# A graph layer in float32 pieces: whole transfers at the start, evacuations ahead of low parts in the first items, the last degrees in fours, W at an item's end, the epilogue one item later

## What is computed

```python
d   = (sum(adj, axis=1) + 1e-9) ** -0.5            # adj 4096 x 4096, degrees by row
H_f = relu((d[:, None] * adj * d[None, :] @ x) @ W_f + b_f)          # x 4096 x 128
H_s = relu((d[:, None] * adj * d[None, :] @ spatial_x) @ W_s + b_s)
a   = sigmoid(concat(H_f, H_s) @ W_att + b_att)    # one number per row
out = layernorm(x + a * H_f + (1 - a) * H_s)       # over the 128 columns
```

## Time and profile before

| | |
|---|---|
| Median of 3 runs | 442.38 us |
| The profiled execution | 443.2 us, its span 441.4 us |
| TensorE | busy 382.8 us (87%), granted clock 0.955 on average |
| VectorE, ScalarE, GpSimd | busy 295.1, 277.8, 200.7 us |
| Transfers | 128.65 MB, mean 291 GB/s; 0.11 MB and 0.21 MB of it instructions |

### The profile page before, as it was taken

How to read it: one execution, slowest core, us unless ns; L and a number is a source line. 1 busy time by engine, 2 the same in 40 slices (tenths; PEclk the granted TensorE clock), 3 DMA queues, 4 the chain that set the end, 5 groups by cost and what they waited for, 6 DMA issues and landing times.

```text
span 441.4 us, 5188 instructions
## 1 busy us (share of the span) xinstructions
PE 382.8 (87%) x1680; PEld 313.5 (71%) x1680; DVE 295.1 (67%) x376; ACT 277.8 (63%) x338; POOL 200.7 (45%) x246
## 2 busy tenths in 40 slices
PE   0699996989979999999999999959999967889850
PEld 0477884868868887888788878748888847768740
DVE  2379957278566957686659834567555775966764
ACT  3778588787577759788888335472525665575323
POOL 1154410119420961195016993340007978578544
PEclk9989998989989999999999999979999996999985
DMA  8999999999799899999999378946553533350011
GB/s 271 417 423 419 418 422 421 420 424 417 307 427 422 318 391 423 422 419 421 421 420 393 102 257 292 408 186 241 202 189 130 171 120 140 102 162 25 12 37 48
DMA packets 25226, 128.65 MB, mean 291 GB/s; under 512 B 2928, under 2 KB 7792, under 8 KB 11376
## 3 DMA queue, kind: packets, MB, share of 16 engines
q1 hardware_dynamic: 25200, 128.33, 73.4%
HBM read 126.22 MB, written 2.10 MB: 291 GB/s over the span
## 4 chain that ended last, share of the span: by engine, by line
PE 33%; DMA 28%; POOL 14%; ACT 9%; DVE 9%; issue 6%; SPq 1%; DVEq 0%; POOLq 0%; ACTq 0%
DMA nat<-in_adj 20%; POOL S L655 10%; PE sums L355 10%; PE sums L356 10%; PE sums L357 10%; DMA raw<-in_At 8%; ACT nat L540 5%; PE sums L368 3%; ACT Ah L526 3%; DVE xs L467 3%; DVE Al L417 2%; DVE st L472 2%; DVE acc L440 1%; POOL xs L662 1%; POOL fin L661 1%
## 5 line engine op out<-in xcount | busy, mean ns | idle before, releaser
L355 PE MATMUL sums<-Ah,Yh 128*128 128x512 f32 x512 | 205.9, 402 | 31.9 <-DVE Yl L428 15.1
L417 DVE TENSOR_TENSOR Al<-raw,Ah 128x2048 fp32r<-128x2048 f32 (+1 forms) x70 | 154.4, 2210 | 108.0 <-ACT Ah L526 107.6
L356 PE MATMUL sums<-Ah,Yl 128*128 128x512 f32 x512 | 203.1, 397 | 0.0
L357 PE MATMUL sums<-Al,Yh 128*128 128x512 f32 x512 | 203.1, 397 | 0.0
L526 ACT ACTIVATE Ah<-raw 128x2048 fp32r<-128x2048 f32 (+1 forms) x70 | 122.9, 1766 | 72.3 <-DMA raw<-in_At 34.8
L355 PEld LDWEIGHTS sums<-Ah,Yh 128*128 128x128 f32 x512 | 98.7, 193 | 56.9 <-DVE Yl L428 15.5
L357 PEld LDWEIGHTS sums<-Al,Yh 128*128 128x128 f32 x512 | 98.4, 192 | 21.3
L356 PEld LDWEIGHTS sums<-Ah,Yl 128*128 128x128 f32 x512 | 98.8, 193 | 20.3
L540 ACT ACTIVATE nat<-nat 128x2048 f32<-128x2048 f32 (+1 forms) x54 | 96.4, 1785 | 15.6 <-DMA nat<-in_adj 14.4
L655 POOL TENSOR_TENSOR S<-S,raw 128x512 f32<-128x512 f32 x48 | 86.6, 1804 | 22.3 <-DMA raw<-in_At 16.2
L633 POOL TENSOR_SCALAR dg<-rs 128x1 f32<-128x1 f32 x31 | 16.9, 546 | 135.1 <-ACT nat L540 120.8
(11 more groups left out here) (35 smaller groups left out, 120.7 us busy)
## 6 DMA issues: line engine op xcount, KB each, us to landing
raw<-in_At SPq DMA_DIRECT2D x62, 1024.0 KB, 9.1
nat<-in_adj SPq DMA_DIRECT2D x46, 1024.0 KB, 10.6
nat<-in_adj SPq DMA_DIRECT2D x12, 512.0 KB, 6.6
xs<-in_xs SPq DMA_DIRECT2D x7, 512.0 KB, 11.3
raw<-in_At SPq DMA_DIRECT2D x8, 256.0 KB, 9.7
out<-xs SPq DMA_DIRECT2D x32, 64.0 KB, 1.7
xs<-in_xs SPq DMA_DIRECT2D x1, 384.0 KB, 11.1
xs<-in_xs SPq DMA_DIRECT2D x1, 128.0 KB, 7.1
```

The costliest lines, as they stand in the source:

```text
L355: pe.matmul(to, Yh[:, t % YRING, hs], high, start=first, stop=False)
L356: pe.matmul(to, Yl[:, t % YRING, hs], high, start=False, stop=False)
L357: mm = pe.matmul(to, Yh[:, t % YRING, hs], low, start=False, stop=last)
L417: dve.tensor_tensor(Al[:, k % SPLITS, a * IB:b * IB], raw[:, k % RAWS, a * IB:b * IB], Ah[:, k % SPLITS, a * IB:b * IB], ALU.subtract).the ...
```

## The change

- Tile 0's parts and item 0 come in whole transfers; x of tile 0 is sent for first. The columns of parts 0, 1 and 3 are shared: ScalarE sums the first half, VectorE the second. Item 1 stays in four pieces.
- Parts 16 to 23 are sent for at items 13, 14, 15, 16, 16, 17, 17, 18; before at 12, 12, 13, 14, 15, 16, 17, 18. The last eight parts are sent for at items 40, 40, 41, 42, 43, 43, 44, 45; before at 43, 43, 44, 44, 45, 45, 46, 46. They hold the first and the last quarter, 1 MB each, and GpSimd leaves out the blocks of items 3, 7, 14 and 15: 32 sums are left.
- VectorE evacuates ahead of the low part in all items up to 15; before up to item 7.
- The degrees of tiles 24 to 27 and 28 to 31 are made four at a time, after GpSimd's loop over the items. Y of tiles 24 to 27 is made at item 46, before at 45.
- W of groups 0 to 5 stands at the end of its item. All four lags are one greater. VectorE's affine stands ahead of the evacuations, and these ahead of the joins. GpSimd has deviation of group g - 1 after mix of group g, for every g. The orders behind the loops are changed to match.

The semaphores of the removed transfers go, and counts follow. The diff, cut to its core:

```diff
     BY_COLUMN = [G - 2, G - 1]
     FULL = (G - 2) * GT
+    OWN_COLUMNS = 2 * G
     parts = {k: [] for k in range(K)}
     for k, r in [(0, 0), (1, 1), (4, 2), (5, 3), (8, 4), (9, 5), (10, 6), (11, 7)]:
         parts[k] = [2 * r, 2 * r + 1]
-    for n in range(16, 2 * FULL):
-        parts[max(12, n - 5) if n < 36 else 31 + (n - 36) * 8 // 11].append(n)
+    for n, k in zip(range(16, 24), [13, 14, 15, 16, 16, 17, 17, 18]):
+        parts[k].append(n)
+    for n in range(24, 36):
+        parts[n - 5].append(n)
+    for n in range(36, 2 * FULL):
+        parts[31 + (n - 36) * 8 // 11].append(n)
     for i in range(2 * GT):
-        parts[FINAL - 5 + i // 2].append(2 * FULL + i)
+        parts[FINAL - 8 + i * 6 // 8].append(2 * FULL + i)
...
     def summed_blocks(k):
 
-        return [j for j, (e, t) in enumerate(items[k]) if k < FINAL and runs[e][0] in BY_COLUMN]
+        return [j for j, (e, t) in enumerate(items[k])
+                if OWN_COLUMNS <= k < FINAL and runs[e][0] in BY_COLUMN]
...
-        return max(whole, free) if r < FULL else max(whole, free, COLLECT + 3)
+        return max(whole, free) if r < FULL else max(whole, free, COLLECT + 4)
...
-    L_MIX, L_LOGIT, L_JOIN, L_NORM = 3, 5, 6, 8
+    L_MIX, L_LOGIT, L_JOIN, L_NORM = 4, 6, 7, 9
...
-    adj_q = adj.rearrange("(r p) (q c) -> r q p c", p=P, q=4)
+    adj_ends = adj.rearrange("(r p) (q c) -> r p q c", p=P, q=4)[:, :, 0::3, :]
...
         def part_summed(eng, n):
 
             eng.wait_ge(rs_act, n + 1)
-            if n < 2:
-                eng.wait_ge(rs_dve, 1 + n)
+            if n in SHARED:
+                eng.wait_ge(rs_dve, SHARED.index(n) + 1)
...
-                if k < 2:
+                if k == 1:
                     for i in range(GT):
                         sp.dma_start(raw[:, k, i * IB:(i + 1) * IB],
-                                     At_v[k, :, i * IB:(i + 1) * IB]).then_inc((raw0_in, raw1_in)[k][i], 16)
+                                     At_v[k, :, i * IB:(i + 1) * IB]).then_inc(raw1_in[i], 16)
                 else:
...
                 r = tile_of(n)
-                if r == 0:
-                    for q in (2 * n, 2 * n + 1):
-                        sp.dma_start(nat[:, n, (q % 2) * (N // 4):(q % 2 + 1) * (N // 4)],
-                                     adj_q[0, q]).then_inc(nat0_in[q], 16)
-                    return
                 if n >= NATS:
                     part_summed(sp, n - NATS)
                 if r < FULL:
                     sp.dma_start(nat[:, n % NATS, :], adj_v[r, n % 2]).then_inc(nat_in[n % NATS], 16)
                 else:
-                    sp.dma_start(nat[:, n % NATS, 0:N // 4], adj_q[r, 3]).then_inc(nat_in[n % NATS], 16)
+                    sp.dma_start(nat[:, n % NATS, :].rearrange("p (q c) -> p q c", q=2),
+                                 adj_ends[r]).then_inc(nat_in[n % NATS], 16)
...
+            sp.dma_start(xs[:, 0:1, :], xs_v[0, :, 0:1, :]).then_inc(x_first, 16)
             for k in range(K):
                 for n in parts[k]:
                     load_part(n)
-                if k == 0:
-                    sp.dma_start(xs[:, 0:1, :], xs_v[0, :, 0:1, :]).then_inc(x_first, 16)
...
+                due = group_at(k, 1)
                 for step, (j, half) in enumerate(sweeps(k)):
-                    if step == GT and group_at(k, 1) is not None:
-                        weigh(group_at(k, 1))
+                    if step == GT and due == TAIL - 1:
+                        weigh(due)
...
+                if due is not None and due < TAIL - 1:
+                    weigh(due)
...
-            for q in (1, 3):
-                dve.wait_ge(nat0_in[q], 16)
-                dve.tensor_reduce(rs0[:, q:q + 1], nat[:, q // 2, N // 4:N // 2], AX.X,
+            def own_share(n):
+                nat_here(dve, n)
+                dve.tensor_reduce(rs0[:, 1, n:n + 1], nat[:, n % NATS, N // 4:N // 2], AX.X,
                                   ALU.add).then_inc(rs_dve, 1)
+
+            own_share(0)
+            own_share(1)
             for k in range(K):
                 ended = [e for e in evac_order if end_item[e] == k - 2]
-                while ended and (k < G or len(ended) == GT):
+                while ended and k < 2 * G:
                     evacuate(ended.pop(0))
+                if len(ended) == GT:
+                    evacuate(ended.pop(0))
+                if k == 1:
+                    own_share(3)
                 low(k)
                 for r in y_at[k]:
                     if r >= 2:
                         y_low(r)
+                g = group_at(k, L_MIX)
+                if g is not None:
+                    for r in of_group(g):
+                        affine(r)
+                for e in ended:
+                    evacuate(e)
                 g = group_at(k, L_JOIN)
                 if g is not None:
                     for r in of_group(g):
                         join(r)
-                for e in ended:
-                    evacuate(e)
-                g = group_at(k, L_MIX)
-                if g is not None:
-                    for r in of_group(g):
-                        affine(r)
+            for r in of_group(TAIL - 3):
+                join(r)
+            for r in of_group(TAIL - 1):
+                affine(r)
             for r in of_group(TAIL - 2):
                 join(r)
             for r in of_group(TAIL - 1):
+                own_logit(r)
+            evacuate(evac_order[-1])
+            join(BY_DVE)
+            for i, r in enumerate(of_group(TAIL)):
                 affine(r)
-            for r in of_group(TAIL - 1):
-                own_logit(r)
-            for r in of_group(TAIL - 1)[:-1]:
-                join(r)
-            evacuate(evac_order[-1])
-            join(BY_DVE + GT - 1)
-            for r in of_group(TAIL):
-                affine(r)
+                if i == 1:
+                    join(r - GT)
+            join(T - GT - 2)
+            join(T - GT - 1)
...
+                if n in SHARED:
+                    act.activation(nat[:, n % NATS, 0:N // 4], nat[:, n % NATS, 0:N // 4], ACT.Copy,
+                                   accum_out=rs0[:, 0, n:n + 1]).then_inc(rs_act, 1)
+                else:
+                    h = n % 2 if r < FULL else 0
+                    act.activation(nat[:, n % NATS, :], nat[:, n % NATS, :], ACT.Copy,
+                                   accum_out=rs[:, r, h:h + 1]).then_inc(rs_act, 1)
...
+            for r in of_group(TAIL - 4):
+                normalise(r)
             for r in of_group(TAIL - 2):
                 logits(r)
             gate(of_group(TAIL - 2))
...
             gate(of_group(TAIL - 1))
-            for r in of_group(TAIL - 2):
-                normalise(r)
             for r in of_group(TAIL):
                 relu(r)
-            for r in of_group(TAIL - 1):
+            for r in of_group(TAIL - 2):
                 normalise(r)
             for rows in PAIRS:
                 gate(rows)
+            for r in of_group(TAIL - 1):
+                normalise(r)
...
+            def last_degrees(rows):
+                a, b = rows[0], rows[-1] + 1
+                part_summed(pool, last_part(b - 1))
+                pool.wait_ge(column_ok, 1)
+                pool.tensor_tensor(less[:, a:b], rs[:, a:b, 0], rs[:, a:b, 1], ALU.add).then_inc(less_ok, b - a)
+                pool.wait_ge(less_ok, b - FULL)
+                pool.tensor_tensor(dg[:, a:b], less[:, a:b], tiny[:, 0:b - a], ALU.add).then_inc(dg_ok, b - a)
+                pool.wait_ge(dg_ok, b)
+                pool.tensor_tensor(D[:, a:b], dg[:, a:b], mhalf[:, 0:b - a], ALU.pow).then_inc(D_ok, b - a)
...
-            degree_of_first()
-            for k in range(FINAL + 1):
-                for r in range(1, T):
+            pool.memset(tiny[:, :], 1e-9).then_inc(pool_const, 1)
+            pool.wait_ge(pool_const, 6)
+            shared_degree(0)
+            shared_degree(1)
+            for k in range(2, FINAL):
+                for r in range(2, FULL):
                     if last_part(r) in parts[k]:
                         degree(r)
                 for j in summed_blocks(k):
                     sum_block(k, j)
+            last_degrees(range(FULL, FULL + GT))
+            last_degrees(range(FULL + GT, T))
             pool.wait_ge(const_in, 16 * 6)
             for g in range(G):
-                if g == TAIL:
-                    deviation(range((g - 1) * GT, g * GT))
                 for r in range(g * GT, (g + 1) * GT):
                     mix(r)
-                if 1 <= g < TAIL - 1:
+                if g >= 1:
                     deviation(range((g - 1) * GT, g * GT))
-                if g == TAIL - 2:
-                    deviation(range(g * GT, (g + 1) * GT))
```

More of the change, by code:

```diff
@@ L211, in build @@
         zero = sb("zero", [P, GT])
+        tiny = sb("tiny", [P, GT])
         sums = ps("sums", [P, 4, 2, IB])
         raw_in = [sem(f"raw_in{i}") for i in range(RAWS)]
[L216 removed]
```

47 lines of the change are left out of this document (16 added, 31 removed).

## The result

| | before | changed |
|---|---|---|
| Median, runs of the comparison | 442.76 us (441.73 to 443.52, 4 runs) | 422.36 us (422.08 to 422.90, 4 runs) |
| The profiled execution | 443.2 us, its span 441.4 us | 422.08 us, its span 420.0 us |

The ratio is 0.9542, with a 95% interval from 0.9519 to 0.9566. The forecast was 423.0 us, in a range from 416 to 432.

A forecast was written before the change was run, and what follows sets the result against it. The prediction took TensorE as busy for most of the span, with the transfer queue setting the pace in the first stages. Gains of 12.6 + 7.4 - 0.7 = 19.3 us gave 423.0 us, range 416 to 432.

The forecast's parts named there:

- Start: Step 1, whole transfers for tile 0 at the kernel's start: 0.9 us gained, between bounds of 0 and 2.0.
- Items up to 33: Step 2, fewer GpSimd sums, later parts 16 to 23, evacuations first: 3.5 us gained, item 8's stop worth 0.
- Last parts: Step 3, the last eight parts at 1 MB each, sent for sooner, their added transfers hidden: 1.1 us gained.
- Degrees and Y: Step 4, last degrees in fours and Y one item later, removing the stop at item 46: 7.1 us gained.
- steps 1 to 4: Everything ahead of the epilogue, from start to degrees and Y: 0.9 + 3.5 + 1.1 + 7.1 = 12.6 us gained.
- Epilogue: Step 5, the reordered last stage: W's waits and lower clock fall from 18.0 to 10.5 us, 7.4 gained.
- The tail: From the last W to the end: 15.4 us become 16.1 as three joins move behind the last affines, cost 0.7.
- That W hardly waits: Rival for the epilogue: only the last W keeps its wait, of 3.7 us; 416 us, chance 0.10.
- That W waits as before: Rival for the epilogue: only the order changes and 18.0 us of loss stay; 430.5 us, chance 0.15.
- That the 4.2 MB aren't hidden: Rival for the last parts: items 40 to 47 take the added 10.0 us of transfers; 433 us, chance 0.12.
- That the lead of step 2 is lost: Rival for items up to 33: later parts or a wait at item 17 eat the lead; 426.5 us, chance 0.08.
- Slower: Rival for the epilogue: later joins delay deviations, mixes and logits, so Ws 2 to 7 wait 6.4 us; 451 us, chance 0.05.

The follow-up runs named there:

- u_evac: The changed kernel with evacuations ahead of the low part only up to item 7 again: 422.23 us, ratio 0.9519 to the kernel before.
- evac17: The changed kernel with evacuations ahead of the low part up to item 17 instead of 15: 422.74 us, ratio 0.9559 to the kernel before.
- u_sums: The changed kernel with GpSimd's 16 dropped block sums restored and only the last quarter of the last eight parts loaded: 425.28 us.
- half_end: The changed kernel loading only the last quarter of the last eight parts, leaving their first quarter out of the degrees: 421.62 us.
- u_step4: The changed kernel with the last eight degrees one by one and Y of tiles 24 to 27 back at item 45: 425.75 us.
- dev_late2: The changed kernel with GpSimd's deviation of group g - 2 behind mix of group g, and ScalarE's normalise later, behind relu and late logits and gates: 418.42 us.
- u_start: The changed kernel with tile 0 and item 0 in pieces again and x of tile 0 in its old place: 423.76 us.
- u_ylate: The changed kernel with only Y of tiles 24 to 27 put back to item 45: 424.50 us, ratio 0.9587 to the kernel before.
- u_parts: The changed kernel with only parts 16 to 23 sent for at their old items: 423.06 us, ratio 0.956 to the kernel before.

## Why the prediction was right

The forecast was 0.6 us over the median, and the mechanism was the forecast one in steps 2, 3 and 5. Part of the nearness is luck: the profiled execution gained 21.4 us of span where the sum said 19.3, as the epilogue and the tail gave more. By its own steps:

1. **Start.** Not contradicted, and too small to measure well: 0.9 forecast, about 0.5 by the bytes of the first 40 us, 0.8 to 1.4 in the times.
2. **Items up to 33.** Right in size. The stop at item 8 was worth 0 (`u_evac`). Item 16's stop was to end at 119.9 - 0.9 = 119.0 and ended at 118.77. Item 32's was to come 3.5 + 0.9 = 4.4 earlier and came 4.7. One reason in it fell, that item 32's evacuation holds the lead: item 25 holds it before, with a chain from a part through eight block sums to its high part, the very order that the step removes before item 17 (`evac17`). Item 32 came as forecast all the same, as that chain too begins at the queue, and item 25's block comes only 1.2 us before its high part. The sums carry this step, 2.9 to 3.7 us in `u_sums`; the part schedule is worth 0.7, less than can be told.
3. **Last parts.** The transfers are hidden (`half_end`), and the hole is gone: ScalarE's wait for item 42's block was 10.13 us, and it waits 2.8 for item 44's now. The gain, called 1.1, is the term that was too small; the lead grew by only 0.3 us from item 32 to the end of item 45, and the rest of this step's gain shows at item 46, in the next.
4. **Degrees and Y.** The stop at item 46 is gone and the end of item 46 comes 12.2 us earlier (12.6 forecast for steps 1 to 4). By place the sum is right here too, 7.2 us gained over item 46. But the 7.1 us were put on the degrees and the Yh alone, and `u_step4` brings back 3.4 (2.3 to 4.5). I had read the whole stop as this step's: "ScalarE's four Yh waited for them, and then came the high part of item 46". Between them stood two row sums of the last parts, 2.1 us, and these belong to step 3, with 0.9 us of earlier column sums at least in part. The sum over both steps was right, since each stop was counted once; the split was not.
5. **Epilogue.** From ScalarE's high part of item 50 to the last W it is 109.1 us (296.21 to 405.27) against 117.6: 8.5 gained, 7.4 forecast (18.0 less 10.5 is 7.5, a slip of 0.1). The chain fell where it was counted: mix of group 2 ends at 16.7 us after item 55 (16.3), the evacuation that releases W 5 at 34.4 (33.8), the last one at 60.1 (61.1). W 5 waits 3.41 (3.0), W 6 0.77 (2.6), the last 2.96 (4.4). W 6's size was off because W 5 itself ran at the lower clock, 3.56 us for 1.8, and came late to it: in the four kernels where W 5 took 2.05 after the same stop, W 6 waits 2.25 to 2.28.

The deviation meets VectorE's subtraction as forecast. GpSimd's timeline in the changed kernel:

```profile
349.19 2.20 POOL L694 TENSOR_TENSOR vare<-mv,epsc 128x4 f32<-128x4 f32 x1 [8.38 <-DVE mv L474]
...
361.75 0.20 POOL L694 TENSOR_TENSOR vare<-mv,epsc 128x4 f32<-128x4 f32 x1
```

VectorE's timeline, the subtraction beside the first of them:

```profile
349.04 2.29 DVE L417 TENSOR_TENSOR Al<-raw,Ah 128x2048 fp32r<-128x2048 f32 x1
```

It costs 2.0 us, and GpSimd's instruction ends with VectorE's. The Trainium skill, "SBUF — State Buffer", SBUF: two separate sides, has an exclusive lock between the two engines, held for a whole instruction; this row agrees. The up to 2 us that it could have cost in the tail did not come: from the last W's affine (406.46) to the end it is 13.5 us, against 13.3 before.

**The tail** was 14.7 us from the last W, where 16.1 was forecast and 15.4 measured before. The 0.7 for the moved joins was mis-sized (0.2), and 0.9 came from the last W's first half, 1.19 us to the affine at 406.46, where it took 2.12 before. That 0.9 is luck of the clock: in the five kernels with this tail whose last W took 3.5 to 3.8 us, the tail is 15.7.

**The rivals.** That W hardly waits: no, 7.1 us stay, and `dev_late2` shows that GpSimd's order, the reason against it, holds W 5. That W waits as before: no. That the 4.2 MB aren't hidden: no, 0.0 to 0.7 us. That the lead of step 2 is lost: no, 4.7 us stand at item 32. Slower: its chain exists and cost W 5 3.4 us, under the 5.0 from which it would decide.

**What stays open.** Undoing one part at a time brings back 1.4 (start), 3.7 (sums), 0.7 (parts), 0 (evacuations), 3.4 (step 4) and 8.4 (epilogue), 17.6 of the 20.4 us by the medians. By the ratios it is 14.5 of 20.3. What is missing can be the earlier last parts, which no run undoes (2.1 us of the stop at item 46 are theirs by the traces, and part of 0.9 more), overlap between the steps, or in part the spread of six differences. Step 5 wasn't tried alone in the kernel before, nor another order of sums and degree ahead of item 25.

## What to carry to other kernels

Ask of every stop whether its stage is set by the engine or by the transfers: 4.3 us at item 8 were worth nothing, and 3.4 at W 5 were worth 2.7 in the trace and 3.9 in the times once two engines' orders were changed together. Where a result can be computed early but is only written out, put it last on every engine that the next critical step passes through; moving it on one engine alone made the kernel slower. Count a stop for all the edits that reach it, and split the gain only after undoing each.

## What the runs showed of the hardware

- **The same stop ahead of W is followed by different clocks.** In nine kernels the last W starts after a stop of 2.96 to 3.02 us, and its 16 matmuls take 2.05 us in `half_end` and `u_start`, 2.59 in the changed kernel, 2.85 in `u_step4`, and 3.49 to 3.78 in `u_ylate`, `evac17`, `u_evac`, `u_parts` and `u_sums`. From 405 to 410 us, where it runs, the granted clock is 0.66 on average in the changed kernel and 0.98 in `half_end`. W 5 after 3.41 to 3.44 us takes 3.56 in the changed kernel and 2.05 in `u_evac` and `evac17`. The price, up to 1.7 us, is paid only where nothing waits next: W 6 begins at 392.04 after the slow W 5 and at 391.94 after the fast one in `u_evac`, with waits of 0.77 and 2.26.
- **GpSimd's power grows with its columns, slower than in proportion.** It takes 0.56 us for 128x1 and 1.02 for 128x4; so wide batches save (7.3 us for 12.4 over eight degrees, each with two instructions that met a subtraction of VectorE), where somebody waits for them.
- **The full queue came to one rate.** With 1 MB blocks the windows from 100 to 125 and from 200 to 225 us show 421 GB/s, the same as the earlier trace rows from 200 to 225; no window shown here is above it.
